# Mamba-2 state-space stage on one Trainium2 core: the next tile's chunk states move from behind the scan to in front of it

## The reference

```python
proj = hidden_states @ in_proj_w.T
gate, xBC, dt = split(proj)
xBC = silu(causal_conv4(xBC))
x, Bm, Cm = split(xBC)
# per head, in chunks of 128 tokens; cs = cumsum(dt * A) in the chunk
scores = (C @ B^T) * exp(cs_l - cs_s) * lower_triangle
Ydiag  = scores @ (x * dt)
states = B^T @ (exp(cs_last - cs) * x * dt)
prev   = running sum over chunks: prev * exp(cs_last) + states
Yoff   = C @ prev * exp(cs)
y = (Ydiag + Yoff + x * D) * silu(gate)
out = (y * rstd * norm_w) @ out_proj_w.T
```

## Time and profile before

| what | value |
|---|---|
| runs | 2485.41, 2486.57, 2487.36 us |
| profiled execution, span from first to last instruction | 2482.8 us |
| median of the runs less that span | 3.8 us |
| PE, DVE, ACT, POOL busy, share of the span | 96%, 72%, 64%, 50% |
| mixer's first and last scan start | 59.6 us, 1544.8 us |
| mean granted clock of PE | 0.986 |

### The profile page before, as it was taken

The page is one execution under the profiler, slowest core; times in us unless marked ns, Lnnn a source line. Parts: engine busy times, 40 slices in busy tenths (PEclk is TensorE's granted clock), DMA queues, the critical chain, the costliest instruction groups (busy, mean ns, idle before and its releaser), DMA issues. The chain is left out here.

```text
span 2482.8 us, 48888 instructions
## 1 busy us (share of the span) xinstructions
PE 2378.8 (96%) x15424; PEld 1368.9 (55%) x15624; DVE 1787.9 (72%) x3234; ACT 1591.7 (64%) x3327; POOL 1232.0 (50%) x986
## 2 busy tenths in 40 slices
PE   6999999999999999999999998879999999999797
PEld 3555555555555555555555555445555555555443
DVE  6777777777777777777777776577777777788522
ACT  7676776776776776776776775265665656656422
POOL 4455555555555556556556459344434343454223
PEclk8999999999999999999999999999999999999999
DMA  7343343343343343343343341230110110100000
GB/s 248 108 129 111 108 128 111 108 133 105 113 132 107 110 133 109 106 137 109 102 140 109 119 151 56 103 124 1 43 43 1 44 44 1 43 18 1 1 0 34
DMA packets 113827, 218.79 MB, mean 88 GB/s; under 512 B 9632, under 2 KB 43040, under 8 KB 111360
## 3 DMA queue, kind: packets, MB, share of 16 engines
q1 hardware_dynamic: 113536, 215.28, 26.6%
HBM read 212.10 MB, written 3.15 MB: 87 GB/s over the span
## 5 line engine op out<-in xcount | busy, mean ns | idle before, releaser
L256 DVE SCALAR_TENSOR_TENSOR xc<-bank,taps,xc 128x511 f32<-128x511 f32 (+2 forms) x384 | 284.7, 742 | 44.6 <-ACT xc L243 27.4
L984 ACT ACTIVATE E<-wq,cst 128x128 f32<-128x128 f32 x1024 | 311.8, 390 | 2.2 <-PEq L298 2.2
L1268 POOL TENSOR_TENSOR xw<-xt,wdec 128x384 f32<-128x384 f32 x128 | 106.4, 832 | 327.3 <-DVE xt L1119 163.7
L1277 POOL TENSOR_TENSOR acc<-acc,sq 128x512 f32<-128x512 f32 x112 | 172.0, 1536 | 186.8 <-ACT sq L996 186.8
L1911 POOL TENSOR_TENSOR qT<-qT,qrot 128x512 f32<-128x512 f32 x64 | 81.3, 1270 | 368.6 <-DVE qrot L1801 368.6
L1161 DVE SCALAR_TENSOR_TENSOR u<-xc,D,bank 128x512 f32<-128x512 f32 x128 | 95.6, 747 | 210.3 <-PE bank L813 198.8
L1100 DVE TENSOR_TENSOR E<-E,cbm 128x1024 f32<-128x1024 f32 x128 | 242.9, 1898 | 0.8
L61 PE MATMUL bank<-xhi,wx 128*128 128x512 f16 x640 | 242.5, 379 | 0.0
L60 PE MATMUL bank<-xlo,wx 128*128 128x512 f16 x640 | 242.5, 379 | 0.0
L59 PE MATMUL bank<-xhi,wx 128*128 128x512 f16 x640 | 242.5, 379 | 0.0
L1263 POOL TENSOR_TENSOR ecs<-ecs,xcC 128x768 f32<-128x768 f32 x128 | 234.1, 1829 | 0.4 <-POOLq L298 0.4
(11 more groups left out here) (237 smaller groups left out, 6299.4 us busy)
## 6 DMA issues: line engine op xcount, KB each, us to landing
wq<-cs_rows SPq DMA_DIRECT2D x128, 512.0 KB, 4.1
ecs<-ecs_rows SPq DMA_DIRECT2D x128, 384.0 KB, 3.6
wx<-in_w_xbc SPq DMA_DIRECT2D x80, 256.0 KB, 2.7
wz<-in_w_z SPq DMA_DIRECT2D x64, 256.0 KB, 2.7
wo<-in_w_o SPq DMA_DIRECT2D x64, 256.0 KB, 4.0
wq<-in_wq SPq DMA_DIRECT2D x8, 1024.0 KB, 5.7
awo<-in_wo SPq DMA_DIRECT2D x8, 1024.0 KB, 5.0
wkv<-in_wkv SPq DMA_DIRECT2D x8, 512.0 KB, 3.7
```

Source lines behind the costliest of these rows:

```text
L256: self.nc.vector.scalar_tensor_tensor(out=dst[:, d:T], in0=self.k.bank[bank][:, 0:T - d], scalar=self.taps[:, bass.ds(g, 1), b, j, 3 - d:4 ...
L984: ins = nc.scalar.activation(E[t.i % 4][:, h, c], sc.csr[t.i % 2][:, h, c * P:(c + 1) * P], ACT.Relu, scale=-1.0, bias=head(sc.cst, t, c, h))
L1277: nc.gpsimd.tensor_tensor(acc[t.b][:], acc[t.b][:], sq[:], ALU.add).then_inc(acc_done, 1)
```

## The change

Within PE's slot, `states(s+1)` is written in front of `scan(s)`. The sum of squares and the x projection then stand right behind the scan. Nothing else differs: the same instructions, waits, semaphores, buffers and DMAs, and no other engine's stream is touched.

```diff
                 def slot(g, m):
                     s = tile_at(g, m)
-                    scan(s)
                     if tile_at(g, m + 1):
                         states(tile_at(g, m + 1))
+                    scan(s)
                     if s.i == 0 and not (isinstance(s.u, int) and s.u == 0):
                         pe.wait_ge(bt_done, s.u + 1)
                         sum_squares(1 - s.b, s.u, s.n)
```

## The result

The change made the kernel slower. Four runs gave 2581.32 to 2585.27 us with a median of 2583.27; the kernel before, beside them, had 2485.99. The ratio is 1.0389, with a 95% interval of 1.0375 to 1.0402. The forecast was 2591.5 us with a range of 2540 to 2635.

What follows compares the result with a forecast made beforehand. PE, busy 96% of the span, was taken to bound the kernel. Losses of 95 (15 units), 2 (i = 0), 3 (loop boundaries) and 5 us (last unit) make 105; 2486.6 + 105 = 2591.5 us, range 2540 to 2635.

Steps and rivals of the forecast that it cites:

- The mechanism: On PE, states placed first wait for POOL's `xw` and hold up the scan, which starts 0.92 us behind its end.
- the sum: Mixer losses over the whole kernel: 95 + 2 + 3 + 5 = 105 us.
- a ring: `y_ready`, `u`, DVE's chain to `xt`, POOL's `xw`, states, scan, `y_ready`: loss in every slot, 1.41 us at i = 2.
- The ring's length: Scan start to end of `xw` 11.24 us; with 0.92 it takes 12.16 us, against PE's own 10.75.
- The order alone: PE's way from last output product to first x product stays 2.76 us: cost 0, -13 to +13 us in all.
- The correction at i = 1: Slots with i = 1: x projection comes 0.66 us sooner, so 0.6 off the 1.13 us loss, leaving 0.5.
- Loop boundaries: 3 us added for the 7 slots behind a loop boundary, where DVE itself starts `u` late.
- The last unit: POOL, busy with the next layer's weights, sets the pace; of 11 us by the same reckoning 5 were kept.
- B: Rival, chance 0.10: DVE's mask escapes POOL's accumulation, shortening the chain by 0.95 us; about 35 us lost, 2521 us.
- the mask's block: DVE's mask on `E` is held by POOL's accumulation; its 2.17 us, against 1.22 in slot 17, was expected to stay.
- C: Rival, chance 0.06: stalls lower PE's clock to half speed; in half of 94 waiting slots, 130 us more, 2720 us.
- D: Rival, chance 0.06: states find `xw` ready ahead of its recorded end; prize 5 us in all, 2481.5 us.

## Why the prediction was right

**The mechanism held as put.** The states wait for `xw`, start 0.06 us behind its end and the scan 0.86 us later: 0.92 us, as the sum had it. The loss comes in every slot, since the chain is a ring. Shortening it on DVE, with PE's stream untouched, took the loss away; lengthening it by 0.66 us lengthened the slots by 0.66. The two slots of 13.34 us in each unit lose nothing. The sum was 105 us, 97 came. Units without a loop boundary lost 6.3 us each, the very number of the prediction, but by luck, since terms were off in both directions:

- *The ring's length*: 12.16 predicted, 12.07 measured. DVE's chain from the scan's start to `xt` is 0.1 us shorter, because the first state is ready when `u` is done. Over five of the eight places, 0.45 us less in a unit.
- *The order alone*: 0 predicted, within 13 us in all either way. It wins 0.09 us in slots that don't wait, the two long ones of a unit. This is PE in slot 27, where `xw` was there in time:

```profile
400.89 0.38 PE L61 MATMUL bank<-wohi,ylo 128*128 128x512 bf16 x1
401.10 0.83 PE L821 MATMUL bank<-xw,bt 128*128 128x128 f32 x6
401.86 0.66 PE L809 MATMUL bank<-E,xt 128*64 128x128 f32 x8
...
403.22 0.39 PE L813 MATMUL bank<-ecs,st 128*64 128x128 f32 x4
403.55 0.39 PE L59 MATMUL bank<-xhi,wx 128*128 128x512 f16 x1
```

  From the last output product to the first x product it is 2.66 us, where the earlier trace rows had 2.76. The switch cost the 0.20 us that I took (the last record of the states starts at 401.10 + 0.83 - 0.275, the scan at 401.86). What failed is the 0.11 us for the projection's weights: the product starts 0.22 us behind the scan's last record, where the states started 0.20 behind it before.
- *The correction at i = 1*: 0.5 us of loss predicted, 1.0 measured. The projection and the tap came sooner as forecast, and the convolution's first step with them, 6.45 us behind the scan instead of 7.12; but the next instruction, `ylo`, was then blocked. The timelines of DVE and of POOL in slot 24, then DVE's row of `ylo` in the same slot before:

```profile
370.40 0.75 DVE L256 SCALAR_TENSOR_TENSOR xc<-bank,taps,xc 128x511 f32<-128x511 f32 x1 [0.61 <-ACT xc L243]
371.07 1.38 DVE L1184 SCALAR_TENSOR_TENSOR ylo<-u,nw,yhi 128x512 f16<-128x512 f32 x1
```

```profile
370.86 1.04 POOL L209 TENSOR_TENSOR wx<-wx 128x512 f16<-128x512 f32 x1
```

```profile
348.83 0.82 DVE L1184 SCALAR_TENSOR_TENSOR ylo<-u,nw,yhi 128x512 f16<-128x512 f32 x1
```

  POOL's split of `wx` runs from 370.86 to 371.90, and `ylo`, which reads two buffers and starts behind it, lasts until 372.45: 1.38 us where it took 0.82 before. Of the 0.67 us won, 0.56 went back, as much as the correction was too large. I had said of the mask that what POOL doesn't block there it blocks later, and hadn't applied it here. No run moved this split; the block of `ylo` is read from the timelines alone.
- *Loop boundaries*: the six units with a boundary inside the loop lost 6.0 us on average where the sum had 7.0. DVE's late start of `u` was counted as if it came on top of the longer slot, but the longer slot seems to hide part of it (no run separates the two): behind the boundaries `u` started 2.2 to 3.0 us after its scan, against 2.9 to 4.1 before. (The prediction counted seven such units; the seventh, from slot 113 on, is code behind the loop. It lost 4.1 us, because the ring is only 11.6 to 11.7 us long there; why DVE's chain is quicker in code outside the loop wasn't tried.)
- *The first slots* weren't in the sum: scan 0 now waits for the states of tile 1, and scan 1 comes 4.32 us later. That this made up for half of what the units lost less than the 100 us of the sum is luck too. *The last unit*: 5 predicted, 4.4 measured.
- *A reading*: the prediction had PE's clock at nine tenths or more in every slice; the first slice of the earlier trace rows is at eight tenths. It lies at the start and has no part in the sum.

**The second wait, for the copy of B,** is the step that was missing. I had counted `bt_done` among the states' waits, and not asked what lies between the turning of B and the states in the new order. It was harmless to the number, as the run with B turned early alone shows, because the ring hid it; without the ring it costs 15 us.

**The rivals.** *B*: a ring without the mask's block does exist and is 1 us shorter (11.04), as POOL's new order shows, but the change doesn't bring it about, since the distances on DVE and ACT from `u` on stay. *C*: the clock stayed at 1.00 in the mixer's common slots, but not by much: 0.66 us more of stall brought it down in ten of them, and the run with only B turned early, whose ring is that of the kernel after, has one such slot, behind one of its longer stalls (1.73 us, slot 68). *D*: the states never found `xw` early in the slots with i = 0, 2, 4. The last unit shows where the new order waits most, and the clock falls behind it:

```profile
1626.28 0.38 PE L61 MATMUL bank<-wohi,ylo 128*128 128x512 bf16 x1
1631.69 1.65 PE L821 MATMUL bank<-xw,bt 128*128 128x128 f32 x6 [5.04 <-POOL xw L1268]
1633.27 1.12 PE L809 MATMUL bank<-E,xt 128*64 128x128 f32 x8
```

There POOL is the bound. `xw` of tile 127 comes late in both kernels; before, scan 126 went ahead of it, now it waits 5 us with it. Scan 127 waits for POOL anyway, which is why the sum kept only half of this.

## What to carry to other kernels

Moving work ahead of the work that covered its input closes a loop, and a loop costs its excess in every turn; the price of a turn is its length less the longest engine's own time, whatever the busy shares say. Before moving a block, list each of its waits and ask for each what stands between the producer and the new place. If the order is worth having, shorten the chain on the engine that feeds it in the same change: here two edits of a few lines turned 97 us of loss into 4 us of gain.

## What was not expected of the hardware

PE's clock fell behind some stalls and not behind others of the same length. In the kernel after and in the runs with the longer ring and with only B turned early, slots 2 to 120 have 47 waits of 1.6 to 2.5 us in front of the states. Behind 11 of them the scan was slow, with the granted clock at 0.58 over four microseconds in the one shown; behind the shorter waits, the common one of 1.15 us among them, none was. Weights of the first product behind a switch from half to full columns cost nothing that can be seen, 0.22 us from start to start with them and 0.20 between the scan and the states. And a two-input instruction on DVE pays for POOL's work wherever it meets it: the mask 0.95 us, `ylo` 0.56.
